# First attention scores of a decoder layer as four side-by-side products of 32 rows, with a new order on every engine

## The reference, cut to what matters

```python
Q = (x @ Wq.T + bq).reshape(b, t, 16, 16)            # 16 heads of 16 columns
attn_logits = einsum('bhtd,lhd->bhtl', Q, latent) / 4  # 64 latent keys for each head
w = softmax(top_k(attn_logits, 4)); out = (w @ latent + V) @ Wo.T + bo
x = layernorm(x + out)
x = layernorm(x + cross_attention(x, ctx))            # 16 heads, 64 context rows
x = layernorm(x + ffn(x))    # two products to 1024, silu gate, one product back; inputs
                             # rounded to 127 steps, weights to -1, 0, 1
```

## Time and profile before

| | us |
|---|---|
| median of 3 runs | 341.52 |
| lowest, highest | 341.06, 342.79 |
| the profiled execution | 342.95 |
| its span, first to last instruction | 341.2 |

### The profile page before, as it was taken

The page is one execution under the profiler, slowest core; times in us unless marked ns, Lnnn a source line. Parts: engine busy times, 40 slices in busy tenths (PEclk is TensorE's granted clock), DMA queues, the critical chain, the costliest instruction groups (busy, mean ns, idle before and its releaser), DMA issues.

```text
span 341.2 us, 6916 instructions
## 1 busy us (share of the span) xinstructions
PE 322.0 (94%) x2245; PEld 232.6 (68%) x2264; DVE 285.6 (84%) x718; ACT 281.7 (83%) x535; POOL 249.9 (73%) x234
## 2 busy tenths in 40 slices
PE   8899999998899999999999999999999999989892
PEld 4677777766667677767777866776768767666341
DVE  2475489999499999998989999898999998798882
ACT  2476888984768778989899789899999898998883
POOL 3274757799297798989958697989489686577661
PEclk9699999999999999999999999999999999999998
DMA  7989830000000002011021102130401222210001
GB/s 214 422 325 386 281 140 0 2 1 3 0 2 1 17 1 46 2 38 41 1 46 37 28 4 46 32 63 1 48 17 32 62 35 52 55 33 16 13 22 46
DMA packets 24852, 22.28 MB, mean 65 GB/s; under 512 B 19824, under 2 KB 22256, under 8 KB 23920
## 3 DMA queue, kind: packets, MB, share of 16 engines
q1 hardware_dynamic: 24816, 21.84, 21.6%
HBM read 15.01 MB, written 2.10 MB: 50 GB/s over the span
## 4 chain that ended last, share of the span: by engine, by line
PE 44%; DVE 24%; issue 12%; POOL 9%; ACT 8%; DMA 2%; SPq 0%; POOLq 0%; DVEq 0%; ACTq 0%
PE small L585 6%; PE wide L550 5%; PE wide L471 3%; PE wide L483 3%; PE wide L534 3%; PE small L458 3%; DVE m L1105 3%; PE small L635 3%; DMA region_r<-in_wqkr 2%; DVE r L1170 2%; PE wide L564 2%; PE wide L609 2%; DVE ch L1236 2%; DVE m L1157 2%; PE small L506 2%
## 5 line engine op out<-in xcount | busy, mean ns | idle before, releaser
L585 PE MATMUL small<-V_sb,PT_sb 128*128 128x256 f32 x256 | 58.1, 380 | 0.3
L585 PEld LDWEIGHTS small<-V_sb,PT_sb 128*128 128x128 f32 x256 | 47.9, 190 | 8.4 <-issue 1.2
L1375 POOL TENSOR_TENSOR Ls<-Ls,m 128x1024 f32<-128x1024 f32 x16 | 31.5, 1967 | 26.1 <-DVE mask L1119 26.1
L550 PE MATMUL wide<-B_sb,x1T 128*128 128x512 f32 x192 | 49.4, 406 | 1.1 <-ACT PT_sb L866 1.0
L550 PEld LDWEIGHTS wide<-B_sb,x1T 128*128 128x128 f32 x192 | 35.2, 188 | 13.0 <-ACT PT_sb L866 2.7
L1440 POOL TENSOR_TENSOR region_c<-region_c,region_q 128x1024 f32<-128x1024 f32 (+1 forms) x17 | 32.6, 1919 | 14.5 <-DVE region_c L1229 12.0
L1105 DVE MAX8 m<-Ls 128x8 f32<-128x64 f32 x256 | 33.9, 210 | 8.9 <-ACT Ls L796 8.7
L1390 POOL TENSOR_TENSOR Ls<-Ls,mask 128x1024 f32<-128x1024 f32 x16 | 38.8, 2427 | 2.4 <-ACT Ls L809 1.8
L1413 POOL TENSOR_TENSOR P<-P,r 128x1024 f32<-128x1024 f32 x16 | 34.0, 2125 | 4.5 <-DVE r L1173 4.5
L1382 POOL TENSOR_TENSOR mask<-mask,r 128x1024 f32<-128x1024 f32 x16 | 30.4, 1902 | 8.4 <-DVE r L1128 8.4
L609 PE MATMUL wide<-tern,region_k 128*128 128x512 bf16 x111 | 28.1, 379 | 1.7 <-issue 0.6
(11 more groups left out here) (189 smaller groups left out, 846.6 us busy)
## 6 DMA issues: line engine op xcount, KB each, us to landing
region_q<-in_wqx SPq DMA_DIRECT2D x1, 2048.0 KB, 17.3
region_c<-in_woTx SPq DMA_DIRECT2D x1, 2048.0 KB, 7.7
out_x<-region_q SPq DMA_DIRECT2D x16, 128.0 KB, 2.0
first<-in_xT SPq DMA_DIRECT2D x7, 256.0 KB, 7.9
region_c<-in_wkcqT SPq DMA_DIRECT2D x1, 1536.0 KB, 11.8
region_r<-in_wqkr SPq DMA_DIRECT2D x1, 1024.0 KB, 8.4
region_r<-in_w1T SPq DMA_DIRECT2D x1, 1024.0 KB, 10.6
region_t<-in_w2T SPq DMA_DIRECT2D x1, 1024.0 KB, 13.1
```

Of the source, the lines that this page charges most:

```text
L550: mm = pe.matmul(ps_L2[:, r * 512:(r + 1) * 512], x1T[:, u, k, :], B_sb[:, s, w, k, r * 512:(r + 1) * 512], start=(u == w == k == 0), stop ...
L585: mm = pe.matmul(ps_O2[:, 0:D], PT2_sb[:, c, :], V_sb[:, c, :], start=(c == 0), stop=(c == PAIRS - 1))
L1375: pool.tensor_tensor(heads(Ls[n % 2][:]), heads(Ls[n % 2][:]), over_heads(m8[:, :, 0:1]), ALU.subtract).then_inc(g_d1, 1)
```

## The change

`L1` issues eight products of 32 rows and 128 columns instead of four of 64 rows and 256 columns. Four of them, at rows 0, 32, 64 and 96, stand side by side in the array and write four banks, half of each of `wide[1]` and `wide[2]`. `lat_k` becomes half as wide, because 32 rows hold only two heads. `copy_L1` reads one half of the scores from each of the two tiles. Each `L1` waits for both tiles. The names of the PSUM tiles are dealt out anew (`V_(0, ...)` moves to `wide[1]`), `sum_2` gets one wait more, and the lists of all five engines are new.

```diff
-        lat_k = sb("lat_k", [P, KD, 4 * L])
+        lat_k = sb("lat_k", [P, KD, 2 * L])
...
+        odd_even = sb("odd_even", [P, 2])
...
-        ps_L1 = wide[1]
...
-        ps_T2T = wide[2]
-        ps_WF = small[1]
+        ps_T2T = wide[1]
+        ps_WF = small[0]
...
-        ps_V = (wide[2], wide[2])
-        ps_T1 = (wide[2], wide[0])
-        ps_A = (wide[1], wide[2])
+        ps_V = (wide[1], wide[2])
+        ps_T1 = (wide[0], wide[1])
+        ps_A = (wide[0], wide[2])
         ps_C = (wide[2], wide[1])
-        ps_Z_last = (wide[0], wide[1])
-        ps_HT_last = (wide[0], wide[2])
+        ps_L1 = (wide[1], wide[2])
+        ps_Z_last = (wide[0], wide[2])
+        ps_HT_last = (wide[2], wide[1])
...
             def L1(n, *freed):

-                bank_of(*freed)
+                for k in range(0, len(freed), 2):
+                    bank_of(*freed[k:k + 2])
...
                 for g in range(KD):
-                    for j in range(2):
-                        mm = pe.matmul(ps_L1[:, j * 512 + g * SEQ:j * 512 + (g + 1) * SEQ],
-                                       QT[b % QRING][j * L:(j + 1) * L, g, q * P:(q + 1) * P],
-                                       lat_k[j * L:(j + 1) * L, g, :], start=True, stop=True)
+                    for j in range(4):
+                        rows = slice(32 * j, 32 * (j + 1))
+                        col = (j % 2) * 512 + g * 2 * L
+                        mm = pe.matmul(ps_L1[j // 2][:, col:col + 2 * L],
+                                       QT[b % QRING][rows, g, q * P:(q + 1) * P], lat_k[rows, g, :],
+                                       start=True, stop=True)
                 mm.then_inc(p_L1, 1)
...
-            warm(9, wide[0]); Q(0); warm(4, wide[0], p_warm, 1); L1(0); T1_(0)
-            T1_(1, p_warm, 2); L1(1, a_L1, 1); Q(1, a_Q, 1); T2_(a_T1, 2); L1(2, a_L1, 2)
-            WB(a_Q, 2); PT1(0, a_T2k, 1); T2T(a_T1, 1); WF(v_WB, 1); A_(0, a_L1, 3)
...
+            warm(9, wide[0]); Q(0); warm(4, wide[0], p_warm, 1); L1(0)
+            warm(2, wide[0], p_warm, 2); T1_(0, p_warm, 3); T1_(1, a_L1, 1); Q(1, a_Q, 1)
+            L1(1, a_T1, 2, a_L1, 1); T2_(a_T1, 1); WF(); PT1(0, a_T2k, 1); T2T(a_L1, 2)
...
-            V_(0, 4, a_V1, 5); X1T(10, v_xlo, 10); O1(11, a_AT, 12); PT1(12, v_sub2, 10)
-            Z_(0, 5, None, a_V0, 5); Z_(1, 5, None, a_L1, 14); WT(12, v_y1, 12)
-            PT2(8, a_PT1, 13); O1(12, a_AT, 13); L1(14, v_g2, 6); L2(10, a_PT2, 9)
...
+            WT(11, v_y2, 8); X1T(10, v_xlo, 10); PT1(12, v_sub2, 10); Z_(0, 5, None, a_V1, 5)
+            O1(11, a_AT, 12); PT2(8, a_PT1, 13); Z_(1, 5, None, a_V0, 5); WT(12, v_y1, 12)
+            O3(4, v_xlo, 11); L2(10, a_PT2, 9); L1(14, v_g2, 6, v_g1, 6); O1(12, a_AT, 13)
...
             def copy_L1(n):
...
-                for j in range(2):
+                for half in range(2):
                     ins = act.activation(
-                        Ls[n % 2][:].rearrange("p (g j n) -> p j g n", g=KD, j=2)[:, j],
-                        ps_L1[:, j * 512:(j + 1) * 512].rearrange("p (g n) -> p g n", g=KD), ACT.Copy)
+                        Ls[n % 2][:].rearrange("p (g h j n) -> p h g j n", g=KD, h=2, j=2)[:, half],
+                        ps_L1[half][:].rearrange("p (j y g n) -> p y g j n", j=2, y=2, g=KD)[:, 0], ACT.Copy)
...
             def spread_lat_k():
...
+                link(dve.tensor_reduce(odd_even[:], head_rows[:].rearrange("p e (j i) -> p i e j", i=2),
+                                       mybir.AxisListType.XY, ALU.add))
                 for g in range(KD):
-                    for e in range(2):
-                        r = slice(e * L, (e + 1) * L)
-                        ins = dve.tensor_tensor(
-                            lat_k[r, g, :].rearrange("p (j l) -> p j l", j=4),
-                            lat_k_raw[r, g:g + 1, :].to_broadcast([L, 4, L]),
-                            head_rows[r, e, :].rearrange("p (j o) -> p j o", o=1).to_broadcast([L, 4, L]),
-                            ALU.mult)
-                    ins.then_inc(c_latk, 1)
+                    dve.tensor_tensor(lat_k[:, g, :].rearrange("p (i l) -> p i l", i=2),
+                                      lat_k_raw[:, g:g + 1, :].to_broadcast([P, 2, L]),
+                                      odd_even[:].rearrange("p (i o) -> p i o", o=1).to_broadcast([P, 2, L]),
+                                      ALU.mult).then_inc(c_latk, 1)
...
             def sum_2(n):

                 dve.wait_ge(a_ex2, n + 1)
+                since(dve, v_sm2, n)
```

More of the change, by code:

```diff
@@ L1024, in _ @@
+            copy_XQ(15); square_h(14); copy_HT(13); tanh(15, 0); square_3(12); tanh(15, 1)
+            whole_h(14); copy_HT(14); square_h(15); square_3(13); whole_h(15, 0); whole_h(15, 1)
+            square_3(14); copy_HT(15, 0); copy_HT(15, 1); square_3(15)
         @block.vector
@@ new lines, in _ @@
+            gaps_4(12); norm_3(2); residual_2(6); top_4(12); sum_4(12); residual_3(3)
+            scale_x(5); gate_1(4); gate_2(4); low_x1(9); residual_2(7); largest_h(4); scale_h(4)
+            sum_2(8); max_2(9); shift_2(9); max_8(13); low_x1(10); largest_x(6); top_4(13)
+            norm_3(3); gaps_4(13); residual_1(11); sum_4(13); scale_x(6); gate_1(5); gate_2(5)
+            sum_2(9); residual_3(4); max_2(10); shift_2(10); residual_1(12); largest_h(5)
+            largest_x(7); scale_x(7); max_8(14); scale_h(5); low_x1(11); residual_2(8)
@@ new lines, in _ @@
+            norm_3(4); gaps_4(14); gate_1(6); gate_2(6); top_4(14); max_2(11); shift_2(11)
+            sum_4(14); low_B(0, 3); gate_1(7); residual_2(9); largest_h(6); sum_2(10)
+            scale_h(6); residual_3(5); largest_x(8); scale_x(8); gate_2(7); residual_1(13)
+            max_8(15); top_4(15); gaps_4(15); norm_3(5); low_B(1, 3); low_B(2, 3); low_B(3, 3)
+            low_x1(12); largest_x(9); sum_4(15); largest_h(7); scale_h(7); sum_2(11)
+            residual_1(14); residual_3(6); scale_x(9); max_2(12); shift_2(12); gate_1(8)
@@ new lines, in _ @@
+            norm_3(6); gate_2(8); low_x1(13); residual_2(10); sum_2(12); residual_3(7)
+            gate_1(9); largest_h(8); max_2(13); scale_h(8); shift_2(13); gate_2(9); low_x1(14)
+            residual_2(11); largest_x(10); norm_3(7); scale_x(10); sum_2(13); largest_h(9)
+            residual_1(15); max_2(14); residual_3(8); shift_2(14); scale_h(9); gate_1(10)
+            residual_2(12); norm_3(8); largest_x(11); scale_x(11); gate_2(10); sum_2(14)
+            low_x1(15); largest_h(10); scale_h(10); largest_x(12); residual_2(13); scale_x(12)
@@ new lines, in _ @@
+            max_2(15); shift_2(15); residual_3(9); gate_1(11); gate_2(11); largest_x(13)
+            sum_2(15); scale_x(13); largest_h(11); scale_h(11); norm_3(9); residual_2(14)
+            residual_3(10); gate_1(12); gate_2(12); largest_x(14); scale_x(14); residual_2(15)
+            largest_h(12); norm_3(10); residual_3(11); scale_h(12); gate_1(13); gate_2(13)
+            largest_x(15); scale_x(15); largest_h(13); scale_h(13); gate_1(14); gate_2(14)
+            norm_3(11); residual_3(12); largest_h(14); scale_h(14); gate_1(15, 0); norm_3(12)
@@ L1324, in _ @@
+            gate_2(15, 0); gate_1(15, 1); gate_2(15, 1); residual_3(13); largest_h(15, 0)
+            largest_h(15, 1); scale_h(15); norm_3(13); residual_3(14); norm_3(14)
+            residual_3(15); norm_3(15)
         @block.gpsimd
```

364 lines of the change are left out of this document (168 added, 196 removed).

## The result

| | before | after |
|---|---|---|
| median us (six runs each) | 342.27 | 339.25 |
| lowest, highest | 341.06, 342.80 | 338.91, 339.64 |
| ratio after / before, 95% interval | | 0.9933 [0.9916, 0.9950] |
| profiled execution, its span | 342.95, 341.2 | 339.06, 337.3 |

The changed kernel is 0.7% faster: 2.3 us by the ratio; the two medians lie 3.0 us apart. The forecast was 338.2 us, 3.3 less than before.

The account below looks back on a forecast made before the run. TE was taken to set the pace for four fifths of the span, VectorE close behind. From 341.52 us, -4.3 for the product and +1.0 for the second tile, all else 0, gave 338.2 us, range 336 to 340.

Parts of the forecast that it names:

- What bounds the kernel: Whole span: TE products fill 94%, VectorE 84%, ScalarE 83%; TE work taken out does not come back in full.
- The product: Score blocks on TE: 0.58 us start to start instead of 1.07, together 7.8 us of TE work saved.
- What of it shows: Of the 7.8 us of TE work, 55%, the score product's share on the chain of waits, shows: -4.3 us.
- Masks, copy, the wait in `sum_2`: VectorE's smaller weight masks, the score copy with other strides, and the added wait for a reciprocal: 0 each.
- `warm(2)`: 0: Two zero products ahead of `T1_`, some 0.4 us, inside 1.51 us in which TE waits for weights: 0.
- Two tiles instead of one, and the new order: Scores hold `wide[1]` and `wide[2]`: +1.0 us, bounds 0 to 12; new lists: -2 to +2, taken as 0.
- The sum and the median: Profiled execution 342.95 - 4.3 + 1.0 = 339.6 us; it lay 1.4 above the median, so median 338.2.
- The clock holds at the start: Rival: clock stays at 2.4 GHz from 10.8 to 17.5 us, some 2.5 us more gain, 335.7 us; chance 0.12.
- The gain is swallowed: Rival: VectorE and ScalarE with their copies decide, TE only gets idle time; 340.7 us; chance 0.2.
- The weight loads decide: Rival: at most two score weight loads overlap, block about 1.06 us, TE gains nothing; 342.5 us; chance 0.08.
- The second tile makes TE wait: Rival: score products wait in TE's list for both tiles, 0.65 us a tile; 347 us; chance 0.14.
- The signs: L471 busy near 10 us, blocks 0.58 apart; PE busy near 313 us, idle under 5 from 100 to 300 us.

Follow-up runs that it names:

- a_64: Kernel after with score products of 64 rows again, its lists, both tiles and all waits kept; 343.38 us, ratio to before 1.0061.
- a_64_nowarm: Kernel after with score products of 64 rows and without the `warm(2)` ahead of `T1_`; 342.66 us, ratio to before 1.0037.
- a_32_twice: Kernel after with each 32-row score product issued twice, the second over the first; 343.62 us, ratio to before 1.0052.
- b_warm: Kernel before with `warm(2)` added ahead of `T1_`; 341.58 us, ratio to before 1.0004.
- a_nowarm: Kernel after without the `warm(2)` ahead of `T1_`; 338.85 us, ratio to before 0.9936.
- after2: Kernel after, unchanged, timed in a second series; 338.86 us, ratio to before 0.9916.
- a_64_one: Kernel after with 64-row score products in `wide[1]` alone, waits for the second tile dropped or set back, lists kept; 343.63 us, ratio to before 1.0045.
- b_64_two: Kernel before, its lists and 64-row products kept, scores in two PSUM tiles, four calls moved; 373.42 us, ratio to before 1.0943.
- a_dve: Kernel after with the VectorE instruction `gaps_4` done twice, 16 added in all; 342.40 us, ratio to before 1.0023.

## Why the prediction was right, and where its steps were not

**What bounds the kernel.** "TE sets the pace for four fifths of the span. VectorE is close behind", and TE work taken out does not come back in full. The runs bear this out from both sides: TE time comes through at 53 to 67%, or 76% by the furthest pair (a_64, a_64_nowarm, a_32_twice), VectorE time at half or more, ScalarE time hardly.

**The product.** The step said 0.58 us a block, "since four products side by side are what L495 has". It is 0.66. For blocks 2 to 15 this makes 14 x 0.41 = 5.7 us instead of 6.9. Block 1 saved 0.4 and not 0.9, since in most executions it never ran at the low clock. Some 6.1 us in place of 7.8, or 6.6 if block 0 is counted. Why 0.66 and not L495's 0.57 no run isolates; the width of the weights, 128 columns against 32, is one difference between the two.

**What of it shows.** The step took the line's share on the chain of waits, 55%, and so 4.3 us. Measured are 3.5 and 4.4 us. The size is right, from a base that was a fifth to a quarter too large and a share that was on the low side. The chain had been read as "often leaves TE although TE is never idle", and that is what the added idle time of after shows: it lies ahead of later products that wait for VectorE, GpSimd and ScalarE. The step also said VectorE would fill 94.4% of the stretch if the whole saving were taken from it. It fills 184.5 of 200 us in after, 92.3%, against 185.1. But the new lists alone had thinned it out, as the same stretch of a_64 shows:

```profile
100.00:300.00 200.00, 195.83 (x1320) 142.87 (x1318) 182.42 (x445) 178.24 (x331) 161.13 (x140) 1.00 0.15 29
```

There it is 182.4 us, 91.2%. So the product made VectorE denser by 1.1 points, about half of the 1.9 that the step had for a full saving.

**Masks, copy, the wait in `sum_2`.** Held. The copy is 597 ns, as before. The masks take 0.7 us in place of 1.7 and stand outside TE's path.

**`warm(2)`: 0.** Held in the median (b_warm 1.0004; a_nowarm 0.9936 against 0.9933). The two products take 0.67 us to the next start (9.15 to 9.82) where the step had 0.4. A delay of `T1_` can't be read: it starts at 9.57 us in a_nowarm, at 9.82 in after and at 9.35 in after2.

**Two tiles instead of one, and the new order.** Here a step failed, though the sum did not. The prediction gave +1.0 to the second tile and 0 to the order. The total of both is +1.3 to +2.1, but a_64_one shows that the order carries most of it: under the new lists the second tile costs at most 1.7 us and may cost nothing. That +1.0 for a tile that is nearly free stood in for a loss of the lists that was put at 0 is luck, as it is that the too large base and the share on the low side made up for each other. The upper bound of 12 us failed too. It was taken from waits of a list that was made for one tile ("the longest that a weight load of L471 waited"), and b_64_two puts the price of the second tile, with the four moved calls, under such a list at 32 us. The lists were renewed for the tiles; the 1 to 2 us that they lose are the price of that, and the two terms should have been one.

**The sum and the median.** The sum put the profiled execution 1.4 us above the median of before. The low clock of its start is the likely reason: another execution of before at the same mean clock, 0.986, took 342.91 us, 1.1 above the median of its series, and the two of a_nowarm with a lower clock 1.8 and 3.4. With the measured sizes, -4.4 and +2.1 (the pair with `warm(2)`) or -3.5 and +1.3 (without) make -2.3 and -2.2. This sum is no check of its own, since both terms come from the same ratios.

**The rivals.** *The clock holds at the start*: it did, but in most executions of before as well, so it is no gain of the change. *The gain is swallowed*: a third to a half is, not all; 340.7 would be a ratio of 0.998, outside both intervals. *The weight loads decide*: four row groups load side by side where L534 had two, and a block's 16 loads are busy 0.54 us instead of 0.95, so no. The price that the Trainium skill (TensorE: Matmul & The Clock Gate, LDWEIGHTS) gives a load by its columns, taken 16 times one after another, was rightly set below the row of L534. *The second tile makes TE wait*: not in this change, at 339 and not 347, yet the mechanism is real and larger than its price said (b_64_two).

**The signs.** L471 (now L475) near 10 us and 0.58: 11.6 and 0.66. PE near 313: 315.6, and 313.2 in after2, whose trace has 17 records fewer. Idle time under 5 us from 100 to 300: 6.2, over the mark and under the 8 of the rivals.

**What stays open.** Which exchange in the new lists costs the 1.3 to 2.1 us was not tried. Nor was the product tried under the old lists without the second tile: as it is written, its four row groups write four banks. No version beats the kernel after; a_nowarm equals it.

## What to carry to other kernels

On a kernel whose engines are 80 to 95% busy under hand-written lists, count the time taken from the busiest engine and expect a part of it (half to three quarters here); the line's share on the chain of waits, 55%, was a fair estimate at the low end. A PSUM tile held in addition can be nearly free or ruinous depending on the order around it (0 to 1.7 us against 32 here), so price tile and order together, and never bound it by the waits of a list that was fitted to the old tiles. Before explaining a stretch at the low clock in one profiled execution, look whether other executions of the same kernel have it.

## What the runs showed of the hardware

**Weight loads of four row groups overlap.** 256 loads of 32 rows by 128 columns, 185 ns each as shown, were busy 34 ns for one, mostly in sets of four that start some 0.11 us apart; with two row groups (L538) it was 60 ns, in pairs 0.105 us apart. Both blocks stream 2048 columns, 1024 for each of two halves or 512 for each of four quarters; the quarters bring the block from 1.07 to 0.66 us, a saving of 0.41 where half would be 0.54. An estimate from a_32_twice says why: eight sets take 1.10 us and four take 0.66, so a set costs 0.11 and 0.22 us a block do not shrink with it.

**VectorE and GpSimd exclude each other in some pairs.** A VectorE instruction with two operands in SBUF (`gaps_4`, 0.22 us) lasted 1.48 us in after and 1.60 and 2.40 in a_dve, each time ending within 0.1 us of the end of a GpSimd instruction. The next one in after, L1160, which reads PSUM, started at 62.85 under GpSimd's L1394 and took its usual 1.22. At a second place in after two VectorE instructions fall under one of GpSimd: L1139, with one operand in PSUM, takes its usual 0.41, and `gaps_4` behind it lasts until GpSimd ends.

```profile
169.03 2.10 POOL L1444 TENSOR_TENSOR region_c<-region_c,region_q 128x1024 f32<-128x1024 f32 x1 [1.60 <-DVE region_c L1233]
170.12 0.41 DVE L1139 TENSOR_TENSOR y_row<-small,wo_bo 128x256 f32<-128x256 f32 x1
170.45 0.77 DVE L1115 TENSOR_TENSOR d<-m 128x64 f32<-128x64 f32 x1
```

The Trainium skill (SBUF — State Buffer, "SBUF: two separate sides") says that VectorE with two SBUF inputs and a GpSimd instruction that reads SBUF share a port pair under an exclusive lock, and the one that comes second waits; the traces agree at these places. One overlap in after is not so plain: at 204.26 us `gaps_4` takes 0.21 while L1379, shown from 204.09 on, takes 2.17 in place of its usual 1.93. I had not looked for it: one such stall made up half of what the added instructions of a_dve cost VectorE, and any new order on these two engines deals such collisions out anew. `gaps_4` is held once in before (1.28 us at 69.76) and four times in after (1.43, 0.66, 1.48, 0.77). Whether that is part of what the new lists cost no run shows; VectorE as a whole is busy less under them, 280.9 us in a_64 against 285.6.
